# One kernel, one change: waits around the steady units of a fused attention and convolution kernel rearranged, and the far block of a Toeplitz convolution as a plain fp32 matmul

## What is computed

```python
h = einsum('bct,bcd->bdt', x, W[condition])          # a 32x32 mix chosen per sample
q_c = h @ Wq_c.T + bq_c                              # 192 wide
q = q_c @ Wq_up.T + bq_up                            # 32 heads x 192
kv = h @ Wkv_c.T + bkv_c                             # 64 nope + 64 rope
attn = softmax(q k^T / sqrt(192)); o = attn @ v      # over the 32 "tokens" of a sample
x = x + (sum over heads of o) @ Wo.T + bo
u = x * mask(length)                                 # per sample
y = causal_conv(u, K) + u * D                        # K: 32 x 512 taps of a state space model
y = y * mask(length)
x = x + y @ dequant(qweight).T + bias                # 6 bit weights
```

## Time and profile before

| | us |
|---|---|
| runs | 829.10, 830.59, 834.56 |
| median of the runs | 830.59 |
| the profiled execution | 834.3 |
| its span, first to last instruction | 832.3 |
| mean granted TensorE clock | 0.987 |

### The profile page before, as it was taken

The page is one execution under the profiler, slowest core; times in us unless marked ns, Lnnn a source line. Parts: engine busy times, 40 slices in busy tenths (PEclk is TensorE's granted clock), DMA queues, the critical chain, the costliest instruction groups (busy, mean ns, idle before and its releaser), DMA issues.

```text
span 832.3 us, 16848 instructions
## 1 busy us (share of the span) xinstructions
PE 775.7 (93%) x6841; PEld 646.0 (78%) x6841; DVE 629.7 (76%) x1131; ACT 416.2 (50%) x724; POOL 279.7 (34%) x270
## 2 busy tenths in 40 slices
PE   5799999979998998999999999999878799999996
PEld 5677778768876876877787778788667599999995
DVE  4376878988898786669576666968989578888885
ACT  2375737544673687375555837555565322222221
POOL 4001312130222129121302312111162387777762
PEclk9999999999999999999999999999999799999999
DMA  9901010201011020101201010202025249888851
GB/s 239 215 32 24 4 30 1 52 4 27 5 47 30 1 52 1 29 2 27 61 1 24 29 30 1 52 2 54 14 89 165 89 94 213 212 214 211 205 131 65
DMA packets 54765, 57.85 MB, mean 70 GB/s; under 512 B 23280, under 2 KB 33312, under 8 KB 54688
## 3 DMA queue, kind: packets, MB, share of 16 engines
q1 hardware_dynamic: 52416, 56.08, 26.8%
q0 software_dynamic: 1056, 0.49, 0.3%
q10 hardware_dynamic: 1216, 0.19, 0.2%
HBM read 44.00 MB, written 8.55 MB: 63 GB/s over the span
## 4 chain that ended last, share of the span: by engine, by line
PE 72%; DVE 17%; POOL 5%; issue 2%; ACT 2%; DMA 1%; SPq 1%; another core or an unknown queue 0%; ACTq 0%; DVEq 0%; POOLq 0%
PE ps L731 24%; PE ps L609 8%; PE ps L610 7%; PE ps L611 7%; PE ps L780 5%; DVE z_low L1446 5%; PE ps L1056 4%; PE ps L1057 4%; PE ps L625 3%; PE ps L806 2%; PE ps L1025 1%; POOL pT_low L530 1%; DVE sc L1431 1%; PE ps L694 1%; DVE sc L1417 1%
## 5 line engine op out<-in xcount | busy, mean ns | idle before, releaser
L530 POOL TENSOR_TENSOR pT_low<-pT,pT_high 128x512 fp32r<-128x512 f32 x60 | 82.4, 1375 | 349.9 <-ACT pT_high L1158 349.9
L1147 ACT ACTIVATE qt<-ps,m_bias 128x512 f32<-128x512 f32 x242 | 155.3, 686 | 77.5 <-PE ps L731 77.5
L731 PE MATMUL ps<-q_high,m_high 64*128 64x512 f32 x768 | 154.3, 396 | 1.7 <-ACT qt L1147 1.2
L731 PE MATMUL ps<-q_high,m_low 64*128 64x512 f32 x768 | 151.1, 387 | 0.0
L731 PE MATMUL ps<-q_low,m_high 64*128 64x512 f32 x768 | 108.5, 387 | 0.0
L731 PEld LDWEIGHTS ps<-q_high,m_high 64*128 64x128 f32 x768 | 73.0, 184 | 23.8 <-issue 5.5
L731 PEld LDWEIGHTS ps<-q_low,m_high 64*128 64x128 f32 x768 | 73.0, 184 | 14.4
L1446 DVE TENSOR_TENSOR z_low<-ps,z_high 128x512 fp32r<-128x512 f32 x128 | 78.3, 683 | 7.6 <-ACT z_high L1168 7.4
L731 PEld LDWEIGHTS ps<-q_high,m_low 64*128 64x128 f32 x768 | 73.1, 184 | 13.2
L1168 ACT CAST z_high<-ps 128x512 fp32r<-128x512 f32 x128 | 65.1, 614 | 15.0 <-PE ps L806 14.6
L1152 ACT ACTIVATE sc<-sc 128x512 f32<-128x512 f32 x60 | 37.7, 632 | 62.4 <-DVE sc L1423 62.3
(11 more groups left out here) (281 smaller groups left out, 1829.6 us busy)
## 6 DMA issues: line engine op xcount, KB each, us to landing
x_in<-in_x SPq DMA_DIRECT2D x16, 512.0 KB, 3.8
x_s<-in_x SPq DMA_DIRECT2D x32, 256.0 KB, 5.6
toep_high<-taps_scratch SPq DMA_DIRECT2D x32, 256.0 KB, 4.7
toep_low<-taps_scratch SPq DMA_DIRECT2D x32, 256.0 KB, 5.7
out<-res SPq DMA_DIRECT2D x32, 256.0 KB, 2.7
c_tok<-ctok SPq DMA_DIRECT2D x64, 64.0 KB, 2.1
wq_nope<-in_L_attn_Wq_up SPq DMA_DIRECT2D x2, 1536.0 KB, 11.7
wq_rope<-in_L_attn_Wq_up SPq DMA_DIRECT2D x4, 384.0 KB, 10.9
```

Of the source, the lines that this page charges most:

```text
L530: pool.tensor_tensor(pT_low_of(u, n), pT_of(u, n), f(pT_high_of(u, n)), ALU.subtract).then_inc(s["pl_done"], 1)
L731: mm = pe.matmul(ps[:, FOLD_BANK[(j // 2) % 2] + e, :], weights[rows, (GH * g + j) // 2, c, :], moving[c][rows, :], start=start, stop=stop)
L1147: act.activation(qt[:, j, :], ps[:, FOLD_BANK[(j // 2) % 2] + j % 2, :], ACT.Identity, bias=m_bias[:, h:h + 1]).then_inc(s["qt_done"], 1)
```

## The change

1. *Start:* on PE, ACT and DVE, `project_ca(0)` and `project_ab(0)` go ahead of `products(0)`, and `project_kv(0)` ahead of `turned_weights(0)`. `scores(0, 0)` no longer waits for `fold_done`; `turn_latent(0)` does.
2. *Angle steps:* the same 48 steps are spread differently. Ahead of `last_head`: unit 2 had 4 and has 7, unit 3 had 11 and has 7, unit 4 had 4 and has 7, unit 5 had 11 and has 7. The middle of units 1 and 5 has one more step each.
3. *Unit 14:* length cast and masks move behind the loop of units, ahead of the first take of unit 15.
4. *Last unit:* the four pieces of a half are handled as two pairs (128x512 instructions on DVE, ACT and POOL). `c_row` moves behind the pieces of unit 14. `values_late(0)` goes ahead of `scores_half(0, n)`, `output(14, 0)` ahead of `scores_half(1, n)`, `turned_wo` and `woT_low` go earlier. `output_last(half)` computes two of four column blocks at a time, after half of `z_low`.
5. *Channels:* the far block (e = 3) is one plain fp32 matmul with 128 columns: a third scratch tensor with unsplit taps, a third DMA per channel of 128x128, a new ACT copy `x1T_far` of 128x128. The zero blocks are gone. PE's order in an iteration is `attention_out(c)`, `convolved(c-2)`, `turned(c-1)`, `projected(c-3)`; DVE does `y(c-2)` ahead of `x1T_low(c-1)`.
6. *Last channels:* `projected` of channels 30 and 31 writes to banks of their own and doesn't wait for `res`; the last one is computed in two halves of columns, with its low part on DVE, and is stored in two halves.

```diff
@@ SP
-            for n in range(2):
+            for n in range(3):
                 sp.dma_start(scratch_taps[n][:, 0:KPAD], zero[:]).then_inc(s["taps_stored"], 16)
...
-                    src = bass.AP(scratch_taps[part].tensor, c * KROW, [[1, P], [1, T]])
-                    sp.dma_start(f(tile[:]), src).then_inc(ring_toep[c % R], 16)
+                    src = bass.AP(scratch_taps[part].tensor, c * KROW, [[1, P], [1, (TT - 1) * P]])
+                    sp.dma_start(f(tile[:, 0:(TT - 1) * P]), src).then_inc(ring_toep[c % R], 16)
+                src = bass.AP(scratch_taps[2].tensor, c * KROW + (TT - 1) * P, [[1, P], [1, P]])
+                sp.dma_start(toep_far[c % R][:], src).then_inc(ring_toep[c % R], 16)
@@ PE, start
+            project_ca(0)
+            project_ab(0)
             pe.wait_ge(s["wk_in"], 16)
             products(0)
-            project_ca(0)
-            project_ab(0)
+            project_kv(0)
             turned_weights(0)
-            project_kv(0)
             products(1)
@@ PE, last unit
+            values_late(0)
             for n in range(4):
                 scores_half(0, n)
-            for n in range(4):
+            for n in range(1, 4):
                 values_late(n)
-            for j in range(2, 4):
-                fold(LAST, 4 * j, 4 * j + 4)
+            fold(LAST, 8, 12)
+            turned_wo()
+            fold(LAST, 12, 16)
+            output(LAST - 1, 0)
             for n in range(4):
                 scores_half(1, n)
-            output(LAST - 1, 0)
-            output(LAST - 1, 1)
-            turned_wo()
-            output(LAST - 1, 2)
-            output(LAST - 1, 3)
+            for n in range(1, 4):
+                output(LAST - 1, n)
             for n in range(4):
                 values_last(n)
-            for n in range(4):
-                output(LAST, n)
+            for half in range(2):
+                output_last(half)
@@ PE, channels
-                for e in range(TT):
-                    first, last = (1, TT + 1 - e) if e < TT - 1 else (0, 2)
-                    out_ = ps[:, 4 + q, (TT - last + first) * P:T]
+                for e in range(TT - 1):
                     rows = slice(e * P, (e + 1) * P)
-                    high, low = (tile[q][:, first:last, :].rearrange("p t b -> p (t b)") for tile in (x1T_high, x1T_low))
-                    mm = three(out_, toep_high[c % R][:, rows], toep_low[c % R][:, rows], high, low, e == 0, e == TT - 1)
+                    high, low = (tile[q][:, 0:TT - e, :].rearrange("p t b -> p (t b)") for tile in (x1T_high, x1T_low))
+                    three(ps[:, 4 + q, e * P:T], toep_high[c % R][:, rows], toep_low[c % R][:, rows], high, low, e == 0, False)
+                mm = pe.matmul(ps[:, 4 + q, (TT - 1) * P:T], toep_far[c % R][:], x1T_far[q][:], start=False, stop=True)
                 mm.then_inc(s["conv_ready"], 1)
...
+            def projected_last():
+                q, bank = (C - 1) % 2, f_bank(C - 1)
+                pe.wait_ge(s["yl_last"], 1)
+                pe.wait_ge(s["x1_done"], C)
+                for n, (weights, width) in enumerate(((wfT_b, HALF + 2), (wfT_a, HALF))):
+                    for k in range(TT):
+                        for part in (y_high[q], y_low[q]):
+                            mm = pe.matmul(ps[:, bank + 1 - n, 0:width], part[:, k, :], weights[:, k, :],
+                                           start=(k == 0 and part is y_high[q]), stop=(k == TT - 1 and part is y_low[q]))
+                    mm.then_inc(s["f_half"], 1)
...
                 if c < C:
                     attention_out(c)
+                if 0 <= c - 2 < C:
+                    convolved(c - 2)
                 if 0 <= c - 1 < C:
                     turned(c - 1)
-                if 0 <= c - 2 < C:
-                    convolved(c - 2)
@@ ACT, channels
-                    act.copy(x1T_high[q][:, 1:, :].rearrange("p t b -> p (t b)"),
-                             ps[:, 2 + q, :]).then_inc(s["x1T_high_done"], 1)
+                    act.copy(x1T_far[q][:], ps[:, 2 + q, 0:P]).then_inc(s["x1T_far_done"], 1)
+                    act.copy(x1T_high[q][:].rearrange("p t b -> p (t b)"), ps[:, 2 + q, :]).then_inc(s["x1T_high_done"], 1)
@@ DVE, units
                 if u == 2:
-                    angles(6, 10)
+                    angles(7, 14)
                 if u == 3:
-                    angles(10, 21)
+                    angles(14, 21)
                 if u == 4:
-                    angles(27, 31)
+                    angles(27, 34)
                 if u == 5:
-                    angles(31, 42)
+                    angles(34, 41)
```

More of the change, by code:

```diff
@@ L436, in _ @@
                 load_x1(c)
-            for c in range(C):
+            for c in range(C - 1):
                 store(c)
@@ L569, in _ @@
                 front_ended(u)
[L570 to L576, removed]
-                    pool.tensor_tensor(c_row[:], c_row[:], s_row[:], ALU.mult).then_inc(s["c_done"], 1)
+            pool.wait_ge(s["row_in"], 32)
+            chain(pool.tensor_scalar(c_row[:], z_row[:], 0.0, 63.0, ALU.max, ALU.min))
+            chain(pool.tensor_scalar(c_row[:], c_row[:], MAGIC, None, ALU.add))
+            chain(pool.tensor_scalar(c_row[:], c_row[:], MAGIC, None, ALU.subtract))
+            chain(pool.tensor_tensor(c_row[:], c_row[:], z_row[:], ALU.subtract))
+            pool.tensor_tensor(c_row[:], c_row[:], s_row[:], ALU.mult).then_inc(s["c_done"], 1)
+            for u in (LAST, NU):
+                for m_ in range(2):
+                    prob_low_two(u, m_)
             pool.wait_ge(s["oh_early"], 1)
@@ L771, in scores @@
                     pe.wait_ge(s["kv_done"], u // 2 + 1)
-                if u == 0 and n == 0:
-                    pe.wait_ge(s["fold_done"], QUADS - 2)
                 if u >= 1:
@@ L868, in output, with output_last @@
                     mm.then_inc(s["out_done"], 1)
+            def output_last(half):
+                pe.wait_ge(s["zl_done"], 8 * LAST + 4 * half + 4)
+                for a in range(GP):
+                    p = GP + a
+                    part = lambda tile: tile[:, 2 * half:2 * half + 2, a, :]
+                    mm = three(ps[:, BO, HALF * half:HALF * half + HALF], wvT_high[:, p, :], wvT_low[:, p, :],
+                               part(z_high), part(z_low), False, half == 1 and a == GP - 1)
+                if half == 1:
+                    mm.then_inc(s["out_done"], 1)
             def tap_products(n):
@@ L1055, in projected @@
                         first, last = k == 0 and part is y_high[q], k == TT - 1 and part is y_low[q]
[L1056 to L1057 removed]
+                        pe.matmul(ps[:, bank, 0:HALF], part[:, k, :], wfT_a[:, k, :], start=first, stop=last)
+                        mm = pe.matmul(ps[:, bank + 1, 0:HALF + 2], part[:, k, :], wfT_b[:, k, :], start=first, stop=last)
                 mm.then_inc(s["f_ready"], 1)
+            def projected_last():
[8 more added lines that the diff above has]
+                    mm.then_inc(s["f_half"], 1)
             for c in range(C + LAG):
@@ L1647, in _ @@
                         dve.sem_inc(s["wf_ready"], 1)
-                    chain(dve.tensor_copy(len_f[:], len_i[:]))
-                    for k in range(TT):
-                        chain(dve.tensor_scalar(mask[:, k, :], len_f[:], l_pos[:, 0:1], float(P * k), ALU.subtract,
-                                                ALU.is_gt))
                 last_head(u)
@@ L1690, in _, with two_rows @@
                     dve.tensor_tensor(taps_low, taps, f(taps_high), ALU.subtract).then_inc(s["taps_done"], 1)
-            for n in range(4):
-                take_scores(LAST, n)
-            below_max(LAST, 0)
-            below_max(LAST, 1)
+            dve.wait_ge(s["len_in"], 16)
+            chain(dve.tensor_copy(len_f[:], len_i[:]))
+            for k in range(TT):
+                chain(dve.tensor_scalar(mask[:, k, :], len_f[:], l_pos[:, 0:1], float(P * k), ALU.subtract, ALU.is_gt))
+            def two_rows(u, m_):
+                return sc_last[:, 2 * m_:2 * m_ + 2, u - LAST].rearrange("p n b a c -> p n (b a) c")
@@ L1712, in _ @@
+            for m_ in range(2):
+                normalised_two(NU, m_)
             for n in range(4):
```

237 lines of the change are left out of this document (147 added, 90 removed).

## The result

The changed kernel takes 803.53 us (median of 4 runs, 801.88 to 804.07), the kernel before 829.85 beside it (825.62 to 834.56): ratio 0.968, 95% interval 0.962 to 0.973, **faster by 26 us**. On two other chips the same pair gave 804.43 against 829.52 and 810.00 against 836.02. The execution profiled after took 804.07, with a span of 802.1.

The account below looks back on a forecast made before the run. TensorE, busy 93% of the span, was taken as the bound, so gains are PE waits, PE work or low clock removed. Terms sum to 27.1 us: profiled 834.3 gives 807.2, 803.5 for the runs; range 796 to 813.

Parts of the forecast that it names:

- Start: Start of the kernel: 5.7 us from projections ahead of `products(0)`, 0.5 from the moved `fold_done` wait; 6.2, bound below 4.6.
- Units 3 and 5: PE waits in `values` behind DVE's angle steps shrink: 4.6 us in unit 3, 3.2 in unit 5.
- handed on: Rival, several places: with PE earlier, the next wait ends late; 814.6, up to 819 us; chance 0.15.
- Unit 14: Length cast and masks leave DVE's way: 1.7 us, with lost clock taken back 3.0 (1.7 to 3.6).
- Last unit: DVE chain after the last scores shortened by merged pairs, halves and moves: 5.0 us gained (1.5 to 8).
- the softmax chain: Last unit, DVE: merged pairs and `woT_low` moved ahead cut it from 12.5 to 9.0 us, 3.5 gained.
- the halves: Last unit: `output_last` in column halves starts after four `z_low` instead of eight, 2.4 us gained.
- the pairs: Last unit: a pair waits for both members and POOL's low part comes as one instruction; about 1.0 us lost.
- the clock: Last unit: of 6.8 us at low clock, 1.0 us is taken back.
- locked ports: Rival, last unit: DVE held for whole GpSimd instructions at two subtractions, 1.2 us less gain, 804.7; chance 0.06.
- Channels: Channel stretch: far block 3.6 us gained, start 1.0 lost, tail 2.5 gained; 5.1 together (2.8 to 8).
- far block no cheaper: Rival, channels: the plain fp32 far block costs 0.36 us, so the 3.6 go, 807; chance 0.05.

Follow-up runs that it names:

- the last column of the table: Stage-by-stage time differences between the first profile of the kernel before (span 832.3 us) and the third profile of the unchanged changed kernel (804.7).
- the first pair: The first profiles of the kernel before and of the changed kernel, spans 832.3 and 802.1 us, compared stage by stage.
- three variants: Changed kernel with angle steps undone (812.94 us), and two versions with masks behind the last `z_low`, last-unit output later, turns first (808.07; with `turned_wo`, `woT_low` later 805.98).
- short `c_row` chain: Changed kernel with POOL's `c_row` chain cut from five instructions to one, leaving out clamping, rounding and zero-point subtraction: 807.33 us (806.30 to 809.81).

## Why the prediction came out, point by point

The median was forecast at 803.5 and came at 803.53. That closeness is partly luck: the differences of the medians, each on one chip, are 26.3, 25.1 and 26.0 us, the sum was 27.1, and the kernel before, from whose 830.59 it was taken, has a median of 836 on another chip. The fairest test of the sum is the last column of the table, where both profiles have DVE's stalls and an early clock: 27.6 against 27.1, with one term clearly wrong and 1.5 in stages that the sum put at nothing.

**Start: right, when the clock rises early.** `project_ca` at 21.5 (21.75 forecast), first `fold` at 35.5 (35.5), `fold(1)` 6.4 earlier (6.2). The third zero store stalled nothing. What the prediction missed is that the early rise, which both profiles of before had, is not given: with the late rise 2.5 us of it go.

**Units 3 and 5: right.** The waits went to 0.9 and 0, and with them the low stretches; outside the first pair, 4.1 and 3.9 to 4.4 against 4.6 and 3.2, together 8.0 to 8.5 against 7.8, and 8.5 when undone. The rest of 0.9 in unit 3 and a stretch in unit 5 that I had taken only into the bound cancel. No new wait came in units 2 and 4: "handed on" did not happen.

**Unit 14: right in both parts.** The wait is 1.9, as forecast; the low stretch is gone in the changed kernel's profiles, 2.9 to 3.0. That it returned in three variants at a wait of the same length shows that the 1.3 us for the clock are likely, not sure.

**Last unit: too high by 1.8, and the step that failed is not in the sum at all.** From the take of the last scores to `attention_out(0)` the changed kernel needs 21.7 us (615.1 to 636.8) against 26.6 (634.93 to 661.54): 4.9 gained, where the terms for the softmax chain, the halves, the pairs and the clock make 3.5 + 2.4 - 1.0 + 1.0 = 5.9. Of the missing 1.0, 0.9 stood in no term: a multiplication that takes 0.69 elsewhere took 1.63 beside POOL's `pT_low_last`.

```profile
622.83 1.26 POOL L541 TENSOR_TENSOR pT_low_last<-pT_last,pT_high_last 128x512 fp32r<-128x512 f32 x1 [7.25 <-ACT pT_high_last L1201]
623.01 1.63 DVE L1753 TENSOR_TENSOR sc_last<-sc_last,row_stat 128x512 f32<-128x512 f32 x1
```

The kernel with the short `c_row` chain has it again, also 1.63 long. From the start of `fold(15)` to that take it needs 30.3 instead of 28.7: 1.6 lost, where I had +0.5 for `values_late(0)` and -1.4 for the two subtractions beside `c_row`, together -0.9. These subtractions took 1.10 and 0.76 us, and 0.69 each with the short `c_row` chain, whose last unit is 0.6 shorter, so they cost 0.5 to 0.6. What is left, 1.0 or a little more, is the masks. I had written, for unit 14, that the masks "move to a place where DVE waits 2 us for scores" and priced them at 1.7. They took 4.3 there with their cast (593.56 to 597.83), so DVE came late for its own scores, and PE waited 2.6 for it. I had counted the port conflict for the subtractions beside `c_row`, and not for the instructions that the change itself puts beside `pT_low`. That is the rival "locked ports" at another place: the mechanism was listed, its victim was not. Moved on, they gave back 1.3 of PE's waits. Whether the +0.5 arrived, no run shows by itself.

**Channels: right, term by term.** Far block 0.14 a period (0.12), 4.1 us instead of 3.6; the start 0.8 (1.0); the tail 16.4 to 13.9, the 2.5 forecast; a period of 4.86 (4.87). The slack of 0.6 for the chain turn, copies, subtract was enough, and "far block no cheaper" is out.

## What to carry to other kernels

Work moved into an idle slot must be priced with its new neighbours: four mask instructions cost 1.25 us in one place and 4.05 in another, as GpSimd was working on SBUF beside them, and the slot of 2 us became a wait of 2.6. Before a sum is compared with a pair of profiles, profile the old kernel twice: here two profiles of the same old kernel lie 7.2 us apart, by stalls and clock for the most part, which is more than any single part of the change was worth. A short far block, padded to 256 fp32r columns, was best replaced by one plain fp32 matmul of 128, not by narrower fp32r ones.

## What the runs showed of the hardware

- Start-to-start times on PE at full clock: fp32r with 256 columns 0.12 us; with 128 columns 0.06, 0.11 and 0.11 for the three of a block, 0.10 in the mean; one plain fp32 matmul of 128 columns 0.22 (two records). Halving the columns of a fp32r matmul from 256 thus saved 0.02 to 0.03 a matmul in place of 0.06. Why was not tried.
- The clock rose between 13.1 and 15.5 us in some executions and between 21.7 and 22.8 in others, for one and the same program too. Later, the same wait of PE was followed by a low stretch (97.8 to 101.2, for one) in one execution and by none in the next: behind the 1.4 us wait in unit 1 in three profiles (the angles undone, the far block undone, the order undone), behind the 1.9 us wait in unit 14 in three. Each costs about 1.3 us. Behind the waits over 3 us in units 3 and 5 it came in five of six cases (not behind unit 5's in the first profile of before).
- Four masks of 128x128 took 1.25 to 1.26 us on DVE where POOL was idle, and 4.05 where it subtracted on 128x512 tiles: three of four then lasted 1.19 to 1.31, as long as POOL's 1.26 to 1.30.
- DVE's turning of scores stalls up to 2.6 us a time in six places in some executions and in none in others, in the units in which POOL issues its gathers; all four kernels on one chip had it. What decides it stays open: no run took the gathers away.
